# A decoder layer on one core: first scores as eight small products in four banks, no products of zeros, a new written order

## The reference, cut to what matters

```python
x = layernorm(x + attn(x))          # 16 heads of 16; 64 latent keys
x = layernorm(x + xattn(x, ctx))    # 16 heads, softmax over 64 context rows
x = layernorm(x + ffn(x))           # ternary weights, activations rounded to 8 bits
# attn: Q = x Wq' + bq, V = x Wv' + bv
#       logits = Q . latent / 4 per head; top 4 of 64; softmax over those 4
#       out = (weights @ latent + V) Wo' + bo
```

## Time and profile before

| what | value |
|---|---|
| median of 3 runs | 341.52 us (341.06 to 342.79) |
| the profiled execution: its own time | 342.95 us |
| its span, first to last instruction | 341.2 us |
| mean granted TensorE clock | 0.986 of full |
| busy: TensorE, VectorE, ScalarE, GpSimd | 322.0, 285.6, 281.7, 249.9 us |

### The profile page before, as it was taken

The page is one execution under the profiler, slowest core; times in us unless marked ns, Lnnn a source line. Parts: engine busy times, 40 slices in busy tenths (PEclk is TensorE's granted clock), DMA queues, the critical chain, the costliest instruction groups (busy, mean ns, idle before and its releaser), DMA issues.

```text
span 341.2 us, 6916 instructions
## 1 busy us (share of the span) xinstructions
PE 322.0 (94%) x2245; PEld 232.6 (68%) x2264; DVE 285.6 (84%) x718; ACT 281.7 (83%) x535; POOL 249.9 (73%) x234
## 2 busy tenths in 40 slices
...
PEclk9699999999999999999999999999999999999998
...
GB/s 214 422 325 386 281 140 0 2 1 3 0 2 1 17 1 46 2 38 41 1 46 37 28 4 46 32 63 1 48 17 32 62 35 52 55 33 16 13 22 46
DMA packets 24852, 22.28 MB, mean 65 GB/s; under 512 B 19824, under 2 KB 22256, under 8 KB 23920
## 3 DMA queue, kind: packets, MB, share of 16 engines
...
## 4 chain that ended last, share of the span: by engine, by line
PE 44%; DVE 24%; issue 12%; POOL 9%; ACT 8%; DMA 2%; SPq 0%; POOLq 0%; DVEq 0%; ACTq 0%
PE small L585 6%; PE wide L550 5%; PE wide L471 3%; PE wide L483 3%; PE wide L534 3%; PE small L458 3%; DVE m L1105 3%; PE small L635 3%; DMA region_r<-in_wqkr 2%; DVE r L1170 2%; PE wide L564 2%; PE wide L609 2%; DVE ch L1236 2%; DVE m L1157 2%; PE small L506 2%
## 5 line engine op out<-in xcount | busy, mean ns | idle before, releaser
L585 PE MATMUL small<-V_sb,PT_sb 128*128 128x256 f32 x256 | 58.1, 380 | 0.3
L585 PEld LDWEIGHTS small<-V_sb,PT_sb 128*128 128x128 f32 x256 | 47.9, 190 | 8.4 <-issue 1.2
L1375 POOL TENSOR_TENSOR Ls<-Ls,m 128x1024 f32<-128x1024 f32 x16 | 31.5, 1967 | 26.1 <-DVE mask L1119 26.1
L550 PE MATMUL wide<-B_sb,x1T 128*128 128x512 f32 x192 | 49.4, 406 | 1.1 <-ACT PT_sb L866 1.0
L550 PEld LDWEIGHTS wide<-B_sb,x1T 128*128 128x128 f32 x192 | 35.2, 188 | 13.0 <-ACT PT_sb L866 2.7
L1440 POOL TENSOR_TENSOR region_c<-region_c,region_q 128x1024 f32<-128x1024 f32 (+1 forms) x17 | 32.6, 1919 | 14.5 <-DVE region_c L1229 12.0
L1105 DVE MAX8 m<-Ls 128x8 f32<-128x64 f32 x256 | 33.9, 210 | 8.9 <-ACT Ls L796 8.7
L1390 POOL TENSOR_TENSOR Ls<-Ls,mask 128x1024 f32<-128x1024 f32 x16 | 38.8, 2427 | 2.4 <-ACT Ls L809 1.8
L1413 POOL TENSOR_TENSOR P<-P,r 128x1024 f32<-128x1024 f32 x16 | 34.0, 2125 | 4.5 <-DVE r L1173 4.5
L1382 POOL TENSOR_TENSOR mask<-mask,r 128x1024 f32<-128x1024 f32 x16 | 30.4, 1902 | 8.4 <-DVE r L1128 8.4
L609 PE MATMUL wide<-tern,region_k 128*128 128x512 bf16 x111 | 28.1, 379 | 1.7 <-issue 0.6
...
## 6 DMA issues: line engine op xcount, KB each, us to landing
region_q<-in_wqx SPq DMA_DIRECT2D x1, 2048.0 KB, 17.3
...
region_r<-in_w1T SPq DMA_DIRECT2D x1, 1024.0 KB, 10.6
...
```

The costliest lines, as they stand in the source:

```text
L550: mm = pe.matmul(ps_L2[:, r * 512:(r + 1) * 512], x1T[:, u, k, :], B_sb[:, s, w, k, r * 512:(r + 1) * 512], start=(u == w == k == 0), stop ...
L585: mm = pe.matmul(ps_O2[:, 0:D], PT2_sb[:, c, :], V_sb[:, c, :], start=(c == 0), stop=(c == PAIRS - 1))
L1375: pool.tensor_tensor(heads(Ls[n % 2][:]), heads(Ls[n % 2][:]), over_heads(m8[:, :, 0:1]), ALU.subtract).then_inc(g_d1, 1)
```

## The change

L1 becomes 8 products, each of 32 rows by 128 columns (2 heads), which write four banks, wide[1] and wide[2]; lat_k halves; copy_L1 reads the four banks. All calls of warm are gone. Which step writes which bank changes with it, and all five lists are new. sum_2 gets one more wait. What each step computes otherwise stays, as does the split of the turns (12 tiles by DMA).

```diff
-        lat_k = sb("lat_k", [P, KD, 4 * L])
+        lat_k = sb("lat_k", [P, KD, 2 * L])
+        odd_even = sb("odd_even", [P, 2])
-        ps_L1 = wide[1]
+        ps_L1 = (wide[1], wide[2])
-        ps_T2T = wide[2]
-        ps_WF = small[1]
+        ps_T2T = wide[1]
+        ps_WF = small[0]
-        ps_V = (wide[2], wide[2])
-        ps_T1 = (wide[2], wide[0])
-        ps_A = (wide[1], wide[2])
+        ps_V = (wide[1], wide[2])
+        ps_T1 = (wide[0], wide[1])
+        ps_A = (wide[0], wide[2])
-        ps_Z_last = (wide[0], wide[1])
-        ps_HT_last = (wide[0], wide[2])
+        ps_Z_last = (wide[0], wide[2])
+        ps_HT_last = (wide[2], wide[1])
...
             def L1(n, *freed):
-                bank_of(*freed)
+                for k in range(0, len(freed), 2):
+                    bank_of(*freed[k:k + 2])
...
                 for g in range(KD):
-                    for j in range(2):
-                        mm = pe.matmul(ps_L1[:, j * 512 + g * SEQ:j * 512 + (g + 1) * SEQ],
-                                       QT[b % QRING][j * L:(j + 1) * L, g, q * P:(q + 1) * P],
-                                       lat_k[j * L:(j + 1) * L, g, :], start=True, stop=True)
+                    for j in range(4):
+                        rows = slice(32 * j, 32 * (j + 1))
+                        col = (j % 2) * 512 + g * 2 * L
+                        mm = pe.matmul(ps_L1[j // 2][:, col:col + 2 * L],
+                                       QT[b % QRING][rows, g, q * P:(q + 1) * P], lat_k[rows, g, :],
+                                       start=True, stop=True)
...
             def copy_L1(n):
-                for j in range(2):
+                for half in range(2):
                     ins = act.activation(
-                        Ls[n % 2][:].rearrange("p (g j n) -> p j g n", g=KD, j=2)[:, j],
-                        ps_L1[:, j * 512:(j + 1) * 512].rearrange("p (g n) -> p g n", g=KD), ACT.Copy)
+                        Ls[n % 2][:].rearrange("p (g h j n) -> p h g j n", g=KD, h=2, j=2)[:, half],
+                        ps_L1[half][:].rearrange("p (j y g n) -> p y g j n", j=2, y=2, g=KD)[:, 0], ACT.Copy)
...
             def spread_lat_k():
+                link(dve.tensor_reduce(odd_even[:], head_rows[:].rearrange("p e (j i) -> p i e j", i=2),
+                                       mybir.AxisListType.XY, ALU.add))
                 for g in range(KD):
-                    for e in range(2):
-                        r = slice(e * L, (e + 1) * L)
-                        ins = dve.tensor_tensor(
-                            lat_k[r, g, :].rearrange("p (j l) -> p j l", j=4),
-                            lat_k_raw[r, g:g + 1, :].to_broadcast([L, 4, L]),
-                            head_rows[r, e, :].rearrange("p (j o) -> p j o", o=1).to_broadcast([L, 4, L]),
-                            ALU.mult)
-                    ins.then_inc(c_latk, 1)
+                    dve.tensor_tensor(lat_k[:, g, :].rearrange("p (i l) -> p i l", i=2),
+                                      lat_k_raw[:, g:g + 1, :].to_broadcast([P, 2, L]),
+                                      odd_even[:].rearrange("p (i o) -> p i o", o=1).to_broadcast([P, 2, L]),
+                                      ALU.mult).then_inc(c_latk, 1)
...
             def sum_2(n):
                 dve.wait_ge(a_ex2, n + 1)
+                since(dve, v_sm2, n)
```

Of TensorE's new list, the start, the places between which tiles 0, 4 to 8 and 11 hand over banks, and the end:

```diff
-            warm(9, wide[0]); Q(0); warm(4, wide[0], p_warm, 1); L1(0); T1_(0)
-            T1_(1, p_warm, 2); L1(1, a_L1, 1); Q(1, a_Q, 1); T2_(a_T1, 2); L1(2, a_L1, 2)
-            WB(a_Q, 2); PT1(0, a_T2k, 1); T2T(a_T1, 1); WF(v_WB, 1); A_(0, a_L1, 3)
+            Q(0); L1(0); T1_(0); T1_(1, a_L1, 1); Q(1, a_Q, 1); L1(1, a_T1, 2, a_L1, 1)
+            T2_(a_T1, 1); WF(); PT1(0, a_T2k, 1); T2T(a_L1, 2); Q(2, a_Q, 2)
+            L1(2, a_T2, 1, a_L1, 2); A_(0, a_PT1, 1); WT(0, v_WF, 1); WB(a_Q, 3)
...
+            PT1(2, a_PT1, 2); C_(0, v_bl, 2); X1T(0, a_Q, 4); O1(1, a_AT, 2); B_(3, 0, a_PT1, 3)
+            WT(2, v_y1, 2); L1(4, v_bl, 3, a_C, 1); L2(0, v_bl, 4); X1T(1, v_xlo, 1)
+            O1(2, a_AT, 3); L1(5, a_L1, 5, a_L1, 5); PT1(3, v_sub2, 1); C_(1, a_L1, 6)
...
+            Q(5, v_xlo, 4); O1(5, a_AT, 6); L1(7, v_bl, 5, v_bl, 6); PT1(6, v_sub2, 4)
+            L1(8, a_L1, 8, a_L1, 8); O2(1, v_y1, 6); B_(2, 1, a_L1, 9); B_(3, 1, a_PT1, 7)
...
+            Z_(0, 6, None, a_L1, 15); X1T(11, v_y3, 5); O2(8, v_y1, 13); PT2(9, v_sub2, 11)
+            Z_(1, 6, None, a_L1, 15); L2(11, a_PT2, 10); B_(0, 3, v_g2, 7)
...
+            XQT(14, v_y3, 12); HT(12, None, v_y2, 16); Z_(0, 14, None, v_g1, 14)
+            Z_(1, 14, None, v_g2, 14); XQT(15, a_qT, 3); HT(13, None, a_hT, 1)
+            Z_(0, 15, 0, a_PT2, 16); O3(12, a_qT, 4); Z_(0, 15, 1); O3(13, v_y3, 13)
+            Z_(1, 15, 0, v_g1, 15); Z_(1, 15, 1); HT(14, None, a_hT, 2); O3(14, v_y3, 14)
+            HT(15, 0, v_g2, 17); HT(15, 1, v_g2, 15); O3(15, v_y3, 15)
```

More of the change, by code:

```diff
@@ L645, in _ @@
[L645 to L698, removed]
@@ L699, in _ @@
-            HT(15, 0, p_warm, 9); HT(15, 1, p_warm, 8); warm(2, wide[1], v_g2, 17)
-            O3(15, v_y3, 15)
+            Q(0); L1(0); T1_(0); T1_(1, a_L1, 1); Q(1, a_Q, 1); L1(1, a_T1, 2, a_L1, 1)
+            T2_(a_T1, 1); WF(); PT1(0, a_T2k, 1); T2T(a_L1, 2); Q(2, a_Q, 2)
+            L1(2, a_T2, 1, a_L1, 2); A_(0, a_PT1, 1); WT(0, v_WF, 1); WB(a_Q, 3)
+            B_(0, 0, a_L1, 3); A_(1, a_L1, 3); Q(3, v_WB, 1); L1(3, v_bl, 1, a_A, 2)
+            PT1(1, a_A, 1); O1(0, a_AT, 1); B_(1, 0, a_L1, 4); B_(2, 0, a_L1, 4); WT(1, v_y1, 1)
@@ new lines, in _ @@
+            PT1(2, a_PT1, 2); C_(0, v_bl, 2); X1T(0, a_Q, 4); O1(1, a_AT, 2); B_(3, 0, a_PT1, 3)
+            WT(2, v_y1, 2); L1(4, v_bl, 3, a_C, 1); L2(0, v_bl, 4); X1T(1, v_xlo, 1)
+            O1(2, a_AT, 3); L1(5, a_L1, 5, a_L1, 5); PT1(3, v_sub2, 1); C_(1, a_L1, 6)
+            WT(3, v_y1, 3); L2(1, a_PT1, 4); X1T(2, v_xlo, 2); O1(3, a_AT, 4); V_(0, 0, a_C, 2)
+            PT2(0, v_sub2, 2); V_(1, 0, a_L1, 6); S3(v_xlo, 3); PT1(4, a_PT2, 1)
+            L1(6, a_V0, 1, a_V1, 1); Q(4, c_mean, 2); L2(2, a_PT1, 5); O2(0, v_y1, 4)
@@ new lines, in _ @@
+            PT1(5, v_sub2, 3); WT(4, v_y2, 1); B_(0, 1, a_L1, 7); PT2(1, a_PT1, 6)
+            X1T(3, a_Q, 5); O1(4, a_AT, 5); L2(3, a_PT2, 2); WT(5, v_y1, 5); B_(1, 1, a_L1, 7)
+            Q(5, v_xlo, 4); O1(5, a_AT, 6); L1(7, v_bl, 5, v_bl, 6); PT1(6, v_sub2, 4)
+            L1(8, a_L1, 8, a_L1, 8); O2(1, v_y1, 6); B_(2, 1, a_L1, 9); B_(3, 1, a_PT1, 7)
+            WT(6, v_y2, 2); X1T(4, a_Q, 6); V_(1, 1, a_L1, 9); V_(0, 1, v_bl, 7)
+            PT2(2, v_bl, 8); O1(6, a_AT, 7); L2(4, a_PT2, 3); O2(2, v_y1, 7); X1T(5, v_xlo, 5)
@@ new lines, in _ @@
+            PT2(3, v_sub2, 5); Z_(0, 0, None, a_V1, 2); Z_(1, 0, None, a_V0, 2)
+            PT1(7, a_PT2, 4); O2(3, v_y2, 3); V_(1, 2, v_g1, 1); WT(7, v_y2, 4); L2(5, a_PT1, 8)
+            L1(9, v_g2, 1, a_V1, 3); O1(7, a_AT, 8); Z_(0, 1, None, a_L1, 10)
+            Z_(1, 1, None, a_L1, 10); O3(0, v_xlo, 6); PT1(8, v_sub2, 6); X1T(6, v_y3, 1)
+            WT(8, v_y1, 8); L1(10, v_g2, 2, v_g1, 2); Q(6, v_xlo, 7); PT2(4, a_PT1, 9)
+            O1(8, a_AT, 9); V_(0, 2, a_L1, 11); Z_(0, 2, None, a_L1, 11); L2(6, a_PT2, 5)
@@ new lines, in _ @@
+            Z_(1, 2, None, a_V0, 3); O2(4, v_y1, 9); PT2(5, v_sub2, 7); B_(0, 2, v_g2, 3)
+            O3(1, a_Q, 7); PT1(9, a_PT2, 6); X1T(7, v_y3, 2); Z_(0, 3, None, v_g1, 3)
+            WT(9, v_y2, 5); L2(7, a_PT1, 10); O2(5, a_AT, 10); X1T(8, v_xlo, 8)
+            L1(11, v_bl, 9, v_g1, 4); O1(9, v_y2, 6); PT2(6, v_sub2, 8); V_(1, 3, a_L1, 12)
+            Z_(1, 3, None, a_L1, 12); PT1(10, a_PT2, 7); B_(1, 2, a_V1, 4); O3(2, v_xlo, 9)
+            B_(2, 2, v_g2, 4); B_(3, 2, a_PT1, 11); WT(10, v_y1, 10); Q(7, v_y3, 3)
@@ new lines, in _ @@
+            V_(0, 3, v_bl, 11); O1(10, a_AT, 11); L1(12, a_V0, 4, v_bl, 10); L2(8, v_bl, 12)
+            O2(6, v_y1, 11); PT2(7, v_sub2, 9); Z_(0, 4, None, a_L1, 13); O3(3, a_Q, 8)
+            PT1(11, a_PT2, 8); Z_(1, 4, None, a_L1, 13); X1T(9, v_y3, 4); O2(7, v_y2, 7)
+            L1(13, v_g2, 5, v_g1, 5); L2(9, a_PT1, 12); V_(1, 4, a_L1, 14); V_(0, 4, a_L1, 14)
+            WT(11, v_y2, 8); X1T(10, v_xlo, 10); PT1(12, v_sub2, 10); Z_(0, 5, None, a_V1, 5)
+            O1(11, a_AT, 12); PT2(8, a_PT1, 13); Z_(1, 5, None, a_V0, 5); WT(12, v_y1, 12)
@@ new lines, in _ @@
+            O3(4, v_xlo, 11); L2(10, a_PT2, 9); L1(14, v_g2, 6, v_g1, 6); O1(12, a_AT, 13)
+            Z_(0, 6, None, a_L1, 15); X1T(11, v_y3, 5); O2(8, v_y1, 13); PT2(9, v_sub2, 11)
+            Z_(1, 6, None, a_L1, 15); L2(11, a_PT2, 10); B_(0, 3, v_g2, 7)
+            Z_(0, 7, None, v_g1, 7); O2(9, v_y2, 9); PT1(13, v_sub2, 12)
+            L1(15, v_bl, 13, v_g1, 8); O3(5, v_xlo, 12); WT(13, v_y2, 10); V_(1, 5, a_L1, 16)
+            Z_(1, 7, None, a_L1, 16); O1(13, a_AT, 14); PT1(14, a_PT1, 14); B_(1, 3, a_V1, 6)
@@ new lines, in _ @@
```

(34 more changed lines are left out.)

265 lines of the change are left out of this document (122 added, 143 removed).

## The result

The changed kernel takes 343.99 us (median of 20 executions, 340.48 to 346.67) against 341.56 us (20, 340.6 to 342.8): ratio 1.0053, 95% interval 1.0032 to 1.0073, so it is slower, by 2.4 us in the medians and 1.8 us by the ratio. An execution over 1.5% above its kernel's fastest (here 346.67 and 346.10 us) is left out of the ratio, but not of the medians. In a second job the changed kernel took 343.52 us against 341.63, ratio 1.0056 (1.0033 to 1.0079), 1.9 us either way. I had forecast 339.0 us, faster. What stands out beside the median is the spread: 6.2 us after, 2.2 us before.

A forecast was written before the change was run, and what follows sets the result against it. TensorE was taken to bound the middle, VectorE 6% behind, and a chain of several engines the last 28 us. From 341.52 us, -5.1 + 1.6 + 1.0 = -2.5 gave 339.0 us, range 334.5 to 345.0.

The forecast's parts named there:

- The first scores: L1, line 471: 0.66 us instead of 1.07 per tile, gain taken as 5.1 us, ends 4.1 and 6.6.
- rival B: Middle of the kernel: VectorE becomes the bound, none of eight L1s' 3.3 us arrives; 342.3 us, chance 0.24.
- (D): L1: the four strips don't work at once, so it stays at 1.09 us; 344.1 us, chance 0.08.
- Four banks and the new order: wide[1] and wide[2], held together by L1: waits for banks cost 1.6 us; the rest of the order costs nothing.
- the places counted: Bank reuses coming too soon: L2(0) 1.0 us short, L1(8) and C_(1) 0.1 each, L2(11) 0.2; 1.4 us together.
- The end without zeros: From 313 us on: the clock falls, O3(15) and HT(15) take longer; cost 1.0 us, ends 0 and 2.6.
- The start without zeros: Before T1: Q(0) and L1(0) run slower but end about when T1's transfer is in; cost nothing, at most 0.4 us.
- Rival C: After T1: clock low another 6.9 us past 17.6 us, +3.4 us; end +1.6 more; 344.0 us, chance 0.16.

The follow-up runs named there:

- the second profile: The changed kernel again, unchanged, in a second job: its profiled execution took 344.18 us, the median of 12 executions 343.52 us.

## Why the prediction was wrong

**The first scores: right in the mechanism, high in the sum.** 0.66 us per L1 was measured as predicted, 0.41 us less per tile. WT, from which this was read, splits the columns (128*32) and L1 the rows (32*128); that both cost the same was assumed, and it came out. The term of 5.1 us was 3.7 us in the new order, under the 4.1 us that I had as its lower end from the chain of waits, for only ten of the 15 tiles' L1s counted. In the old order a like cut in TensorE's work was worth 1.3 us: rival B's mechanism may have part of the truth there, though no run shows that it is VectorE that holds the path. The new order is what lets the rest through. (D) fell: the loads of four strips, each of 128 columns, start 7 ns apart in the trace and do overlap. The Trainium skill (TensorE: Matmul & The Clock Gate, on LDWEIGHTS), by which a load's time goes by its columns, agrees for one load (185 ns for 32 by 128 here, 188 to 190 ns for 128 by 128); it doesn't forbid that four run side by side.

**Four banks and the new order: right in size, partly by luck.** 1.6 us predicted, 1.3 measured (old L1 in the new order against the kernel before). Of the places counted, 1.4 us together, 2.8 us showed in the profile: L2(0) cost 1.35 instead of 1.0 us and C_(1) 1.2 instead of 0.1; L2(11) showed 0.25 against 0.2, and L1(8) nothing. TensorE's idle time is 11.8 us where I expected 8 to 10, and its busy time fell by 15.3 us (322.0 to 306.7), not by 19.

**The end without zeros: right.** 1.0 us predicted; 1.3 us measured (340.57 against 339.23). O3(15) at half the clock was most of the term; it takes 1.88 us in the profile without the end's zeros and 1.06 us with them.

**The start without zeros: this step failed.** The prediction has "Cost nothing, at most 0.4 us", and that the clock was low around T1 "all the same, zeros or not". I had looked only at whether Q(0) and L1(0) end before T1's transfer. They do, T1 starts at 9.6 to 9.9 us in both profiles of the changed kernel. What they leave behind, in most executions, is a clock that is at 1.2 GHz under T1 and part of Q(1). From there to 310 us TensorE is nearly never idle, so the 3.0 us (343.52 against 340.57) arrive whole. And the row I leaned on was not usual: the profiled execution before had a mean clock of 0.986 and took 342.95 us, 1.4 us over the median, while in the second job's 17 executions it was 0.994 to 1.0. With the nine zeros ahead, every profile has the full clock by 8 us, so a later fall does show in the mean. The zeros normally kept the clock up; the one execution that I saw was one in which they had not. The gap between 342.95 and 341.52, which I wrote down and set aside, was the sign of it. As a price it would have been too low: the old order covers part of such a start, and the new one lets all of it through.

Together: -3.7 + 1.3 + 1.3 + 3.0 = +1.9 us, which is 343.52 - 341.63; the four are differences between neighbouring kernels, so they must add up, and what they show is where the 1.9 us come from. Rival C, which had a chance of 0.16, came nearest: its price of 3.4 us for a low stretch of 6.9 us is what the second profile shows. Its place was off, for the clock row isn't low past 20 us: the stretch is the one of the earlier trace rows, not one more behind it, and what was new is that it comes in most executions. That its sum of 344.0 us fits is partly luck: it had 2.6 us for the end (measured 1.3) and 5.1 us for L1 (3.7). The Trainium skill's rule (TensorE: Matmul & The Clock Gate, Part 1, on what is actually happening) that the low clock is the default and that activity releases it was the right warning, at the start rather than at the end: T1 took 3.08 us with four products of zeros ahead of L1(0) and 5.58 us without them.

What stays open: why the clock falls in one execution of the same kernel and not in the next. The zeros change how often, and no run here shows what decides in a given execution. Nor is it shown why the changed kernel with all its zeros still falls in five of 18 executions (a mean of 0.991 or less), while the kernel before, with the same 13 at the start, stayed at 0.994 or more in all 81 of the later jobs, and the version with the old L1 in all its 12.
